# GpSimd drains behind every sixth gather, in place of a memset behind each, in a wide-and-deep recommender kernel

## The chip, the cores and the metric

The kernel runs on one core of one Trainium2 chip. The metric is the device time of one launch in microseconds (us), as the median of several runs. Times inside the kernel come from one profiled execution.

## The reference

The batch has 2048 samples. A sample has 13 dense numbers and eight categorical indices s0 to s7 into tables with 125000, 25000, 12500, 375, 375, 1000, 500 and 100 rows. Each table i has an embedding `Ei` (64 numbers a row) and a weight `wi` (one number a row). Two more weight tables, `wc0` and `wc1`, are indexed by crossed pairs of indices. Everything is float32.

```python
wide = dense @ Wd_wide
for si, wi in zip(S, w):
    wide = wide + wi[si]
wide = wide + wc0[S[3] * 375 + S[4]]
wide = wide + wc1[S[5] * 500 + S[6]]
deep_in = concatenate([dense @ Wd_deep] + [Ei[si] for Ei, si in zip(E, S)], axis=1)   # 2048 x 576
h = relu(deep_in @ W1)      # 512 wide
h = relu(h @ W2)            # 256 wide
return bias + h @ W3 + wide
```

## The kernel before, in words

The batch is cut into four blocks of 512 samples (`BLOCKS`), and each block into four tiles of 128 (`BT`), 16 tiles in all (`TILES`). Each engine has its own program, written out by hand; the engines meet only at semaphores.

**GpSimd (POOL in the profile), lines 308 to 357.** The three large tables are read by indirect DMA, here called gathers. One gather brings 128 rows, one row to a partition. For every tile there are two gathers into `x_pair` (tables 0 and 1, line 333) and one into `x_two` (table 2, line 341), so 12 for each block and 48 for the batch. After them come the gathers of single weights into `cross` (line 351): ten for the first crossed table (its first six tiles are looked up by matmul instead) and 16 for the second. That makes 74 gathers, numbered 1 to 74 in this document in the order of their issue. The first 12, those of block 0, follow one another directly. Behind each of the 61 gathers from number 13 to number 73 stands a `pause` (lines 322 to 326): it waits until the pause before it has finished, and then runs a memset of 128x320 float32 on a tile `pause_sb` that nothing reads.

**Who waits for gathers.** TensorE (PE) turns the gathered rows of block b by transposes at line 755, behind waits on `rows_gathered[b][0]` (for `x_pair`) and `rows_gathered[b][1]` (for `x_two`). VectorE (DVE) waits for all of them at lines 686 and 687, for the ten of the first crossed table at line 693, and for the 16 of the second at line 701. Line 702 then adds the last crossed weights into `result`, and SyncE stores `result` (line 305).

**The other tables.** The five small tables are looked up by matmul. DVE builds one-hot matrices in SBUF, 19 instructions of 128x512 for each block (line 517), and PE multiplies them with the tables (line 730). DVE does this for block 0 at the start, for block 1 at about 24 to 42 us, and for later blocks as their turn comes.

**The two layers.** PE multiplies in three passes (high by high, high by low, low by high: lines 786 to 788) to keep float32 accuracy. ScalarE (ACT) writes the high part of a layer's result after its relu (line 392), DVE the low part (line 542), and PE's second layer (line 819 on, called `layer2`) waits for both. At the end of the kernel ACT applies the last relu (line 401), DVE weighs it with W3 (lines 551 and 560), PE sums over the partitions (line 843, `layer3`), and DVE adds all of it up (lines 700 and 702).

Of the kernel before, what the change touches and what calls it, by code (L numbers as in the profile page):

```python
# [6 lines left out]
P = 128  # L7
# [10 lines left out]
NG, NL, NF = len(GATHERED), len(LOOKED_UP), len(FIELDS)  # L18
ROW = D + 1
CROSSES = [(3, 4), (5, 6)]  # L20
NX = len(CROSSES)
SPLIT = 3

TILES = BATCH // P
BLOCK = 512
BT = BLOCK // P
# [66 lines left out]
def program(nc, index, dense_t, big, small, small_w, wc, wc_rows, wd_rep_t, wd_wide, w1, w2, w3, bias, out):  # L93
    f32, bf16, f16, i32 = mybir.dt.float32, mybir.dt.bfloat16, mybir.dt.float16, mybir.dt.int32
# [5 lines left out]
    with ExitStack() as ctx:  # L100
        def sb(name, shape, dt):
            return ctx.enter_context(nc.sbuf_tensor(name, shape, dt))
# [4 lines left out]
        def sem(name):  # L107
            return ctx.enter_context(nc.semaphore(name))
# [63 lines left out]
        h2 = sb("h2", [P, M2, BLOCK], f32)  # L172
        wide_deep_look = [sb(f"wide_deep_look{h}", [P, BLOCK], f32) for h in range(2)]
        ones = sb("ones", [P, 1], f32)
        pause_sb = sb("pause_sb", [P, 320], f32)

        wide = sb("wide", [P, TILES], f32)
        wide_rows = sb("wide_rows", [P, TILES], f32)
# [48 lines left out]
        w2_high, w2_low = sem("w2_high"), sem("w2_low")  # L227
        rows_gathered = [[sem(f"rows_gathered{b}_{k}") for k in range(2)] for b in range(BLOCKS)]
        cross_gathered = [sem(f"cross_gathered{c}") for c in range(NX)]
        paused = sem("paused")  # L230
        onehot_ready = sem("onehot_ready")
        io_full = sem("io_full")
        io_act = sem("io_act")
# [74 lines left out]
        @block.gpsimd  # L308
        def _(pool):
            nc.gpsimd.memset(zero[:], 0.0).then_inc(zero_ready, 1)  # L310
            nc.gpsimd.iota(row_id[:], pattern=[[P, max(CHUNKS)]], base=0, channel_multiplier=1,
                           allow_small_or_imprecise_dtypes=True).then_inc(row_id_ready, 1)
            nc.gpsimd.iota(col_id[:], pattern=[[1, XPAD]], base=0, channel_multiplier=0,
                           allow_small_or_imprecise_dtypes=True).then_inc(col_id_ready, 1)
            pool.wait_ge(zero_ready, 1)
            for m in (ident16, ident):
                nc.gpsimd.affine_select(out=m[:], in_=zero[:], compare_op=ALU.not_equal, fill=1.0, base=0,
                                        pattern=[[-1, P]], channel_multiplier=1).then_inc(ident_ready, 1)
            pool.wait_ge(ident_ready, 2)
            nc.gpsimd.memset(look_w_parts[:], 0.0).then_inc(look_w_zeroed, 1)  # L320
            nc.gpsimd.memset(ones[:], 1.0).then_inc(ones_ready, 1)
            def pause(n):

                if n:
                    pool.wait_ge(paused, n)
                nc.gpsimd.memset(pause_sb[:], 0.0).then_inc(paused, 1)  # L326

            pool.wait_ge(gather_index_ready, 1)
            pauses = 0
            for b in range(BLOCKS):  # L330
                for t in range(b * BT, (b + 1) * BT):
                    for g in (0, 1):
                        nc.gpsimd.indirect_dma_start(  # L333
                            out=x_pair[:, t, g * ROW:(g + 1) * ROW], out_offset=None, in_=big[g],
                            in_offset=bass.IndirectOffsetOnAxis(ap=idx_gather[:, g, t:t + 1], axis=0),
                        ).then_inc(rows_gathered[b][0], 16)
                        if b > 0:
                            pause(pauses)
                            pauses += 1
                for t in range(b * BT, (b + 1) * BT):  # L340
                    nc.gpsimd.indirect_dma_start(  # L341
                        out=x_two[:, t, :], out_offset=None, in_=big[2],
                        in_offset=bass.IndirectOffsetOnAxis(ap=idx_gather[:, 2, t:t + 1], axis=0),
                    ).then_inc(rows_gathered[b][1], 16)
                    if b > 0:
                        pause(pauses)
                        pauses += 1
            pool.wait_ge(cross_index_ready, 1)
            for c in range(NX):
                for t in range(XTILES if c == 0 else 0, TILES):  # L350
                    nc.gpsimd.indirect_dma_start(  # L351
                        out=cross[:, c, t:t + 1], out_offset=None, in_=wc[c],
                        in_offset=bass.IndirectOffsetOnAxis(ap=idx_cross[:, c, t:t + 1], axis=0),
                    ).then_inc(cross_gathered[c], 16)
                    if (c, t) != (NX - 1, TILES - 1):
                        pause(pauses)
                        pauses += 1

        @block.scalar
        def _(act):  # L360
# [613 lines left out]
```

## Time and profile before

| what | us |
|---|---|
| three runs | 128.6, 130.53, 131.19 |
| their median | 130.53 |
| the profiled execution, its own time | 129.13 |
| its span, first to last instruction | 127.3 |
| busy in the span: PE, weight loads, POOL, DVE, ACT | 117.8, 89.2, 104.8, 80.7, 57.1 |

The span begins with the first instruction that the profile shows. All times of rows below are counted from there. The time of an execution is its span and something around it, here 1.8 us. Busy time of PE overlaps from one matmul to the next, so that the distance of their starts says more than their durations. The profile shows a gather of GpSimd for as long as GpSimd itself works at it; the transfer goes on behind it.

### The profile page before, as it was taken

The numbers are of one execution on the slowest core, as the hardware profiler recorded it, in microseconds if no ns is written. First come the engines' busy times: TensorE is split into PE (matmuls) and PEld (weight loads), VectorE is DVE, ScalarE is ACT, GpSimd is POOL, SyncE is SP. The second block draws the span as 40 slices with busy tenths as digits, with TensorE's granted clock in tenths as the row PEclk, the third lists the DMA queues.
The fourth block names the chain that finished last, engine by engine and source line by source line (L and its number), as shares of the span: only waits on it lengthen the run. The fifth ranks groups of instructions, "written<-read, shape, count | busy, mean of one in ns | idle before, by whom it ended". The sixth has DMA issues, their size and how long they took to land.

```text
span 127.3 us, 1843 instructions
## 1 busy us (share of the span) xinstructions
PE 117.8 (92%) x630; PEld 89.2 (70%) x630; DVE 80.7 (63%) x188; ACT 57.1 (45%) x100; POOL 104.8 (82%) x146
## 2 busy tenths in 40 slices
PE   6979999988999999999999999999999999999710
PEld 2443886646688885788788885787888867888710
DVE  2695996998999604975999025695995040257510
ACT  3599777456946052345462151509170432063200
POOL 6488888888899889888898888898898888888800
PEclk9999999999999999999999999999999999999965
DMA  3957766668922322223233322200000000000000
GB/s 118 344 60 248 147 178 74 133 89 323 290 21 24 26 21 21 21 19 23 21 26 20 21 20 22 21 0 0 6 0 0 0 3 0 6 0 0 0 3 0
DMA packets 6049, 7.48 MB, mean 59 GB/s; under 512 B 2755, under 2 KB 3939, under 8 KB 6040
## 3 DMA queue, kind: packets, MB, share of 16 engines
q0 software_dynamic: 2368, 1.62, 17.6%
q1 hardware_dynamic: 3240, 5.03, 12.1%
q10 hardware_dynamic: 432, 0.72, 1.6%
q8 instruction: 5, 0.08, 0.2%
q14 instruction: 4, 0.03, 0.1%
HBM read 7.17 MB, written 0.19 MB: 58 GB/s over the span
## 4 chain that ended last, share of the span: by engine, by line
POOL 79%; issue 11%; DMA 4%; POOLq 1%; DVE 1%; DVEq 0%
POOL x_pair L333 26%; POOL pause_sb L326 21%; POOL cross L351 18%; POOL x_two L341 14%; DMA idx_raw<-in_index_dram 2%; DMA cross<-in_wc_dram,idx_cross 2%; POOLq L100 1%; DVE idx_wrap L497 0%; DVE idx_sum L499 0%; DVE idx_look L502 0%; DVE result L702 0%; DVE idx_gather L502 0%; DVEq L701 0%
## 5 line engine op out<-in xcount | busy, mean ns | idle before, releaser
L517 DVE TENSOR_SCALAR onehot<-idx_bc,row_id 128x512 fp32r<-128x512 f16 x76 | 39.4, 583 | 3.7 <-PE io_ps L742 2.6
L333 POOL DMA_INDIRECT x_pair<-in_rows_dram,idx_gather x32 | 33.2, 1038 | 8.0 <-issue 6.2
L351 POOL DMA_INDIRECT cross<-in_wc_dram,idx_cross x26 | 25.4, 978 | 4.3 <-issue 4.3
L326 POOL MEMSET pause_sb<- 128x320 f32 x61 | 26.6, 437 | 0.0
L786 PE MATMUL l_ps<-xt_hi,w_hi 128*128 128x512 f32 x64 | 25.8, 404 | 0.2 <-DVE xt_lo L537 0.2
L788 PE MATMUL l_ps<-xt_hi,w_lo 128*128 128x512 f32 x64 | 25.1, 392 | 0.0
L787 PE MATMUL l_ps<-xt_lo,w_hi 128*128 128x512 f32 x64 | 25.0, 390 | 0.0
L730 PE MATMUL io_ps<-onehot,table_hl 128*128 128x512 f32 x76 | 21.0, 406 | 0.1
L375 ACT CAST xt_hi<-io_ps 64x512 fp32r<-64x512 f32 x20 | 11.6, 580 | 19.8 <-PE io_ps L730 19.6
L537 DVE TENSOR_TENSOR xt_lo<-io_ps,xt_hi 128x512 fp32r<-128x512 f32 (+1 forms) x8 | 5.5, 688 | 23.6 <-ACT xt_hi L388 23.6
L341 POOL DMA_INDIRECT x_two<-in_rows_dram,idx_gather x16 | 17.7, 1104 | 3.2 <-issue 3.2
L730 PEld LDWEIGHTS io_ps<-onehot,table_hl 128*128 128x128 f32 x76 | 14.1, 189 | 3.3 <-ACT idx_bc L363 0.3
L401 ACT ACTIVATE h<-l_ps 128x512 f32<-128x512 f32 (+1 forms) x9 | 5.0, 551 | 23.7 <-PE l_ps L788 23.7
L542 DVE SCALAR_TENSOR_TENSOR h_lo<-l_ps,h_hi 128x512 fp32r<-128x512 f32 x16 | 10.2, 683 | 6.9 <-ACT h_hi L392 6.9
L786 PEld LDWEIGHTS l_ps<-xt_hi,w_hi 128*128 128x128 f32 x64 | 12.0, 188 | 3.4 <-DVE xt_lo L537 0.6
L788 PEld LDWEIGHTS l_ps<-xt_hi,w_lo 128*128 128x128 f32 x64 | 12.0, 188 | 2.7
L787 PEld LDWEIGHTS l_ps<-xt_lo,w_hi 128*128 128x128 f32 x64 | 12.1, 188 | 2.3
L786 PE MATMUL l_ps<-h_hi,w_hi 128*128 128x512 f32 (+1 forms) x36 | 13.4, 372 | 0.1
L788 PE MATMUL l_ps<-h_hi,w_lo 128*128 128x512 f32 (+1 forms) x36 | 13.3, 370 | 0.0
L787 PE MATMUL l_ps<-h_lo,w_hi 128*128 128x512 f32 (+1 forms) x36 | 13.2, 368 | 0.0
L376 ACT CAST xt_lo<-io_ps 64x512 fp32r<-64x512 f32 x20 | 11.7, 583 | 0.5
L392 ACT ACTIVATE h_hi<-l_ps 128x512 fp32r<-128x512 f32 x16 | 9.0, 599 | 4.5 <-PE l_ps L788 3.9
(89 smaller groups left out, 132.4 us busy)
## 6 DMA issues: line engine op xcount, KB each, us to landing
idx_bc<-idx_dram SPq DMA_DIRECT2D x3, 640.0 KB, 6.2
table<-in_wc_rows_dram SPq DMA_DIRECT2D x1, 564.0 KB, 4.1
w_sb<-in_w_dram ACTq DMA_DIRECT2D x2, 256.0 KB, 4.6
x_pair<-in_rows_dram,idx_gather POOLq DMA_INDIRECT x32, 3.6
w_sb<-in_w_dram SPq DMA_DIRECT2D x2, 256.0 KB, 3.5
w_sb<-in_w_dram SPq DMA_DIRECT2D x1, 512.0 KB, 4.1
dense_stack<-dense_dram SPq DMA_DIRECT2D x3, 156.0 KB
table<-in_small_dram SPq DMA_DIRECT2D x1, 416.0 KB, 3.8
```

The source lines that it names most:

```text
L326: nc.gpsimd.memset(pause_sb[:], 0.0).then_inc(paused, 1)
L333: nc.gpsimd.indirect_dma_start(out=x_pair[:, t, g * ROW:(g + 1) * ROW], out_offset=None, in_=big[g], in_offset=bass.IndirectOffsetOnAxis(a ...
L341: nc.gpsimd.indirect_dma_start(out=x_two[:, t, :], out_offset=None, in_=big[2], in_offset=bass.IndirectOffsetOnAxis(ap=idx_gather[:, 2, t: ...
L351: nc.gpsimd.indirect_dma_start(out=cross[:, c, t:t + 1], out_offset=None, in_=wc[c], in_offset=bass.IndirectOffsetOnAxis(ap=idx_cross[:, c ...
L375: nc.scalar.copy(xt_hi[b % 2][to, g, :], bank[0:D, :]).then_inc(io_act, 1)
L376: nc.scalar.copy(xt_lo[b % 2][to, g, :], bank[D:2 * D, :]).then_inc(io_act, 1)
L517: nc.vector.tensor_scalar(onehot[:, CHUNK0[i] + c, :], idx_bc[:, b % (BLOCKS - 1), i, :], row_id[:, c:c + 1], None, ALU.is_equal).then_inc ...
L542: nc.vector.scalar_tensor_tensor(out=h1_lo[:, m, :], in0=l1_ps[m][:], scalar=0.0, in1=h1_hi[:, m, :].bitcast(f32), op0=ALU.max, op1=ALU.su ...
L730: last = nc.tensor.matmul(io_bank(use)[:], table_hl[:, c, :], onehot[:, c, :], start=c == CHUNK0[i], stop=c == CHUNK0[i] + CHUNKS[i] - 1)
L786: nc.tensor.matmul(dst, w_hi, a_hi, start=start, stop=False)
L787: nc.tensor.matmul(dst, w_hi, a_lo, start=False, stop=False)
L788: return nc.tensor.matmul(dst, w_lo, a_hi, start=False, stop=stop)
```

## The change

The tile `pause_sb` and the semaphore `paused` go, and so do the 61 memsets and the waits between them. In their place `rest` counts the gathers. Behind the gathers whose number is at least 12 (`NG * BT`, the end of block 0) and a multiple of 6, it issues one `drain` on GpSimd: behind gathers 12, 18, 24, 30, 36, 42, 48, 54, 60, 66 and 72, 11 drains in all. The gathers, their order and their semaphores stay.

```diff
-        pause_sb = sb("pause_sb", [P, 320], f32)
...
-        paused = sem("paused")
...
-            def pause(n):
-
-                if n:
-                    pool.wait_ge(paused, n)
-                nc.gpsimd.memset(pause_sb[:], 0.0).then_inc(paused, 1)
+            def rest(n):
+
+                if n >= NG * BT and n % 6 == 0:
+                    nc.gpsimd.drain()
 
             pool.wait_ge(gather_index_ready, 1)
-            pauses = 0
+            gathers = 0
             for b in range(BLOCKS):
                 for t in range(b * BT, (b + 1) * BT):
                     for g in (0, 1):
...
                         ).then_inc(rows_gathered[b][0], 16)
-                        if b > 0:
-                            pause(pauses)
-                            pauses += 1
+                        gathers += 1
+                        rest(gathers)
...
                     ).then_inc(rows_gathered[b][1], 16)
-                    if b > 0:
-                        pause(pauses)
-                        pauses += 1
+                    gathers += 1
+                    rest(gathers)
...
                     ).then_inc(cross_gathered[c], 16)
-                    if (c, t) != (NX - 1, TILES - 1):
-                        pause(pauses)
-                        pauses += 1
+                    gathers += 1
+                    rest(gathers)
```

## Rows read from the trace of the kernel before

**Rows 1.** The chain of waits that ended last: shares of the span, by line.

```profile
POOL x_pair L333 26%; POOL pause_sb L326 21%; POOL cross L351 18%; POOL x_two L341 14%; DMA idx_raw<-in_index_dram 2%; DMA cross<-in_wc_dram,idx_cross 2%; POOLq L100 1%; DVE idx_wrap L497 0%; DVE idx_sum L499 0%; DVE idx_look L502 0%; DVE result L702 0%; DVE idx_gather L502 0%; DVEq L701 0%
```

**Rows 2.** Timeline of the end: start us, us, engine, line, operation.

```profile
120.03 0.95 POOL L351 DMA_INDIRECT cross<-in_wc_dram,idx_cross  x1 [0.17 <-issue]
...
120.95 0.61 PE L843 MATMUL deep_ps<-ones,wide_deep_look 128*128 128x1 f32 x4 [0.65 <-DVE wide_deep_look L560]
121.59 0.17 DVE L700 TENSOR_TENSOR wide_deep<-wide_bias,deep_ps 128x16 f32<-128x16 f32 x1 [0.70 <-PE deep_ps L843]
122.49 0.17 DVE L702 TENSOR_TENSOR result<-wide_deep,cross 128x16 f32<-128x16 f32 x1 [0.72 <-DMA cross<-in_wc_dram,idx_cross]
```

**Rows 3.** By stretches of 10 us: length, busy of each engine, PE clock, DMA share, GB/s.

```profile
20.00:30.00 10.00, 9.46 (x75) 6.30 (x74) 8.35 (x18) 5.69 (x11) 8.43 (x12) 1.00 0.63 106
...
40.00:50.00 10.00, 10.00 (x55) 8.04 (x57) 4.93 (x10) 2.72 (x5) 8.85 (x14) 1.00 0.29 23
```

**Rows 4.** Timeline of POOL: gathers of block 0 without memsets, then with them.

```profile
4.51 1.27 POOL L333 DMA_INDIRECT x_pair<-in_rows_dram,idx_gather  x1 [1.81 <-DVE idx_gather L502]
6.09 1.17 POOL L333 DMA_INDIRECT x_pair<-in_rows_dram,idx_gather  x1 [0.30 <-issue]
...
21.61 0.94 POOL L341 DMA_INDIRECT x_two<-in_rows_dram,idx_gather  x1 [0.30 <-issue]
22.86 0.95 POOL L333 DMA_INDIRECT x_pair<-in_rows_dram,idx_gather  x1 [0.31 <-issue]
23.80 0.38 POOL L326 MEMSET pause_sb<- 128x320 f32 x1
24.35 0.95 POOL L333 DMA_INDIRECT x_pair<-in_rows_dram,idx_gather  x1 [0.16 <-issue]
25.30 0.55 POOL L326 MEMSET pause_sb<- 128x320 f32 x1
```

**Rows 5.** Timeline of DVE: one-hots in block 0, one-hots under memsets, the low part behind.

```profile
5.87 2.46 DVE L517 TENSOR_SCALAR onehot<-idx_bc,row_id 128x512 fp32r<-128x512 f16 x6 [1.05 <-ACT idx_bc L363]
...
30.70 2.54 DVE L517 TENSOR_SCALAR onehot<-idx_bc,row_id 128x512 fp32r<-128x512 f16 x5
...
33.17 2.47 DVE L542 SCALAR_TENSOR_TENSOR h_lo<-l_ps,h_hi 128x512 fp32r<-128x512 f32 x4
```

**Rows 6.** Timeline of PE: the start of layer2 of blocks 0 and 1, a turn.

```profile
33.48 0.39 PE L788 MATMUL l_ps<-xt_hi,w_lo 128*128 128x512 f32 x1
33.99 0.47 PE L786 MATMUL l_ps<-h_hi,w_hi 128*128 128x512 f32 x1
...
46.43 0.60 PE L755 MATMUL io_ps<-ident,x_pair 128*128 128x128 f32 x4
...
60.90 0.39 PE L788 MATMUL l_ps<-xt_hi,w_lo 128*128 128x512 f32 x1
61.28 0.47 PE L786 MATMUL l_ps<-h_hi,w_hi 128*128 128x512 f32 x1
```

**Rows 7.** The first operation of the kernel's own program on POOL.

```profile
0.74 0.20 POOL L310 MEMSET zero<- 128x128 f32 x1 [0.29 <-POOLq L961]
```

**Rows 8.** Issues of DMAs; the last number is the median us from issue to landing.

```profile
x_pair<-in_rows_dram,idx_gather POOLq DMA_INDIRECT x32, 3.6
...
cross<-in_wc_dram,idx_cross POOLq DMA_INDIRECT x26, 2.3
```

**Rows 9.** Timeline of PE: three-pass matmuls, the first two rows without memsets.

```profile
16.07 0.39 PE L787 MATMUL l_ps<-xt_lo,w_hi 128*128 128x512 f32 x1
...
19.02 0.39 PE L788 MATMUL l_ps<-xt_hi,w_lo 128*128 128x512 f32 x1
...
38.00 0.40 PE L786 MATMUL l_ps<-xt_hi,w_hi 128*128 128x512 f32 x1
...
40.53 0.40 PE L788 MATMUL l_ps<-xt_hi,w_lo 128*128 128x512 f32 x1
...
58.40 0.39 PE L786 MATMUL l_ps<-xt_hi,w_hi 128*128 128x512 f32 x1
```

## The prediction

> **What bounds the kernel now.** I read the chain of waits first. It puts 79% of the span on GpSimd: 26 + 18 + 14 for the three kinds of gathers and 21 for the memsets between them [rows 1]. Taken alone this says that 61 memsets cost a fifth of the time. The end of the timeline says how much of it counts. Gather 74 starts at 120.03, its data releases the last addition (L702) at 122.49. But the other chain is just as late: PE's last sums start at 120.95, and DVE adds them at 121.59 (L700) [rows 2]. So GpSimd is the last of two chains that end almost together. I then read the stretches of 10 us: PE is busy 9.46 of 10 us from 20 to 30, and 10.00 in each of the eight from 40 to 120, at a granted clock of 1.00 [rows 3]. That is the second bound. It takes no gain from GpSimd unless PE itself waited for something that the memsets delayed.
>
> **What GpSimd gains.** From gather 13 at 22.86 to gather 74 at 120.03 there are 61 steps in 97.17 us, 1.59 each [rows 2, 4]. A step is a gather of 0.95, a memset of 0.38 or 0.55, and 0.16 idle. Without a memset gathers stand 1.25 apart where DVE builds no one-hots (21.61 and 22.86, and the two steps before): 0.94 and 0.30 idle [rows 4]. Removing a memset of 0.38 therefore gives back only 0.24 where DVE is quiet. Where DVE builds one-hots, gathers of block 0 took more: 1.17 at 6.09, and the step from 4.51 to 6.09 is 1.58 [rows 4]. I price this from block 0 as a whole. Its 12 steps from 4.51 to 22.86 took 18.35 us, against 12 x 1.25 = 15.0, so 3.35 us more, in a stretch with 19 one-hots: 0.18 us for each one-hot. The other three blocks have 57, hence 10.1 us. Gather 74 would then start at 22.86 + 61 x 1.25 + 10.1 = 109.2, without the drains. The bounds are 22.86 + 76.3 = 99.1 (one-hots cost nothing) and, at block 0's own mean step of 1.53, 22.86 + 93.3 = 116.2.
>
> **What the drains cost.** The trace of before shows no drain. On POOL nothing stands behind a drain but the next gather, and behind that all later ones. Below, a drain costs nothing: GpSimd is idle 0.30 between two gathers anyway. Less than nothing is excluded, as it takes no work away. Above, it would hold the next gather until the transfers in flight have landed. That is 3.6 us after the issue of a row gather and 2.3 after one into `cross` [rows 8]; with 0.30 of idle the step becomes 3.9 or 2.6 instead of 1.25, so 2.65 or 1.35 more. I take 0.3 us, the idle time of POOL where its sequencer went from one part of the program to the next [rows 7], since all that the row shows is a sequencer that starts an empty engine again. 11 x 0.3 = 3.3, and gather 74 starts at 112.5.
>
> A drain is a different thing from a wait for data by the Trainium skill too: PSUM — Partial Sum Buffer, "Engine vs sequencer instructions", says that a drain waits for the engine to be fully idle, and Perfetto Trace Analysis, "DMA Instruction — SWDGE (GPSIMD)", that an indirect DMA is over for GpSimd when its descriptors are written, before its data has moved. By both, the low price holds and the high one does not; no run here shows it yet.
>
> **How much of this reaches the end.** Gather 74 at 112.5 lands at 114.8, before L700 at 121.59, so L702 waits for L700 alone. L700 takes 0.17, and with a few hundredths between them L702 starts at 121.81 instead of 122.49 [rows 2]: 0.68 us less. All else of the 7.5 us that GpSimd wins lies beside PE and gives nothing. GpSimd may lose 6.7 us against my figure (120.03 - 0.68 - 0.13 = 119.2, less 112.5; the 0.13 comes below) before it matters again, which is 0.6 us for each drain on top of the 0.3.
>
> **What PE gains through DVE.** The memsets slow DVE as DVE slows them. Six one-hots of block 0 took 2.46 us, 0.41 each; five under memsets took 2.54, 0.51 each [rows 5]. For 57 of them that is some 6 us of DVE. Does PE wait for it? PE is busy throughout from 40 us on [rows 3]. One place remains: layer2 of block 0 starts 0.51 behind the matmul before it (33.48 to 33.99), that of block 1 0.38 (60.90 to 61.28) [rows 6]. The low part that it needs (L542) began at 33.17, right as those five one-hots came to their end at 33.24, with no idle time of DVE before it [rows 5]: it had been queued behind them. With faster one-hots it falls to 0.38 as in the later blocks: 0.13 less. The idle PE time from 20 to 30 belongs to ACT's copies and to a DMA, which do not change. Bounds: 0 and 0.3 (to the plain distance of 0.23).
>
> The Trainium skill describes this port: SBUF — State Buffer, "SBUF: two separate sides", says that a DVE operation in a two-port mode and a GpSimd operation lock each other out for a whole instruction. The slower one-hots and the memsets of 0.55 instead of 0.38 agree. The same section says that GpSimd cannot write descriptors until such a DVE operation ends, which speaks against the change: it is the third rival below.
>
> **The sum.** 129.13 (the profiled execution) - 0.68 - 0.13 = 128.3; a step behind each chain may take some of it back, and I say 128.4. The median of the three runs is 1.4 above the profiled execution, so it matters whose spread that is. PE's chain is fixed work with no idle time. GpSimd's chain adds up 61 steps that meet DVE or do not (memsets of 0.38 or 0.55). If GpSimd is what made the runs of 130.53 and 131.19 long, PE's chain caps them all near 128.4, and the fastest run, 128.6, is such a run already. I go by that. Own range 127.8 to 129.4.
>
> **The rivals.**
> 1. The spread is not GpSimd's. Then the gain is 0.8 from 130.53: 129.7. For it: nothing in one profile shows what another run did. Against: 128.6 is so near to PE's floor.
> 2. Slower: a drain waits for landings. The place is the tail. Seven drains behind row gathers cost 2.65 and four behind `cross` 1.35: 23.9. Gather 74 then starts at 109.2 + 23.9 = 133.1, or at 123.0 if the waits swallow the cost of the one-hots. The time is 129.13 + 3.0 to 13.1, so 132 to 142, middle 137. It decides from 0.9 us a drain. PE is not starved before: gather 20, the last of block 1's `x_pair`, starts at 22.86 + 7 x 1.53 + 2 x 2.65 = 38.9, lands at 42.5, and PE turns it only at 46.43 [rows 6]. Against it: the 0.30 idle between gathers shows that GpSimd itself does not need the landing.
> 3. Slower: gathers stand still while DVE builds one-hots, now that DVE meets no memset. 57 x 0.41 = 23.4 us lost: 22.86 + 76.3 + 23.4 + 3.3 = 125.9, 5.9 late, 135.0. Against: in block 0 the gather at 6.09 ran within the burst of one-hots from 5.87 to 8.33 and took 1.17 [rows 4, 5].
> 4. Faster: the memsets write SBUF and slow PE's reads. Matmuls start 0.227 apart without memsets (13 steps from 16.07 to 19.02) and 0.230 with them (11 from 38.00 to 40.53). If that 1.3% were theirs, PE's 96 us from gather 13 to its end shrink by 1.2: 128.4 - 1.2 = 127.2. Against: they are 0.227 apart from 58.40 to 60.90 too, with memsets [rows 6, 9].
>
> **How the numbers follow.** The forecast gets 0.60, rival 1 0.17, rival 2 0.11, rival 3 0.04, rival 4 0.08. A measurement of this kernel tells about 2% from no change, so faster means below 127.9 and slower above 133.1. Faster: rival 4 and the lowest part of the forecast, 0.08 + 0.08 = 0.16. Slower: rivals 2 and 3 and a little for a drain of unforeseen price, 0.17. Within 2%: 0.67. The range goes from 127.5 to 131.0: it holds the forecast and rival 1 and leaves out most of rivals 2 to 4.
>
> **What would show it.** Right: the chain of waits of the changed kernel ends through PE, L843 and L700; gather 74 starts between 105 and 117; a gather behind a drain starts 0.3 to 0.9 behind the one before it; one-hots in later blocks take 0.48 as in block 0; L702 starts about 0.2 behind L700; layer2 of block 0 starts 0.38 behind its predecessor. Wrong: gather 74 later than 119, L702 waiting for `cross` again, steps of 3 us and more behind gathers 12, 18, 24; PE with idle time or another distance of matmuls; or a spread of runs as wide as before.

## The result, and the profile after the change

The changed kernel takes 146.81 us (median of 4 runs, 143.68 to 149.53) against 130.51 for the kernel before (median of 4 runs, 128.6 to 131.19). The ratio is 1.1134, with a 95% interval of 1.093 to 1.1338; ratios here and below leave out the executions of a kernel that took over 1.5% longer than its fastest, so this one is lower than 146.81 / 130.51. The forecast of 128.4 and its range up to 131.0 are both missed, on the side of the second rival. The profiled execution took 149.53 and is the longest of the four; sums below are made inside it.

The page of the kernel after: its span, two rows of the 40 slices, the chain of waits by engine and by line, and two groups (the columns of a group are busy us, mean ns of one, idle before).

```profile
span 147.7 us, 1793 instructions
...
PE   6799999989999999999999999999999972000000
...
POOL 5678781687187438708726852852853746737640
...
POOL 48%; issue 35%; POOLq 11%; DMA 3%; DVE 1%; DVEq 0%
POOL x_pair L330 24%; POOL cross L346 14%; POOLq L323 11%; POOL x_two L337 10%; DMA idx_raw<-in_index_dram 2%; DMA cross<-in_wc_dram,idx_cross 2%; POOLq L100 0%; DVE idx_sum L493 0%; DVE idx_wrap L491 0%; DVE idx_look L496 0%; DVE result L696 0%; DVE idx_gather L496 0%; DVEq L695 0%
...
L511 DVE TENSOR_SCALAR onehot<-idx_bc,row_id 128x512 fp32r<-128x512 f16 x76 | 31.3, 480 | 3.8 <-PE io_ps L736 2.7
...
L696 DVE TENSOR_TENSOR result<-wide_deep,cross 128x16 f32<-128x16 f32 x1 | 0.2, 174 | 21.9 <-DMA cross<-in_wc_dram,idx_cross 21.9
```

PE works without a longer pause until the 34th slice and then has nothing left, while GpSimd goes on in bursts. The memsets' 21% of [rows 1] are gone, and "issue" (time in which the engine waited for nothing that the profile shows) with 35% and POOLq (GpSimd's sequencer, here at the drains of L323) with 11% stand in their place. L696 (L702 of [rows 2]) waits 21.9 us for the gathers.

The timeline of POOL of the kernel after, around its first two drains and its ninth (columns as in [rows 2]; the bracket is the idle time before):

```profile
21.80 0.95 POOL L337 DMA_INDIRECT x_two<-in_rows_dram,idx_gather  x1 [0.30 <-issue]
27.19 2.82 POOL L330 DMA_INDIRECT x_pair<-in_rows_dram,idx_gather  x1 [4.45 <-issue]
30.32 0.95 POOL L330 DMA_INDIRECT x_pair<-in_rows_dram,idx_gather  x1 [0.30 <-issue]
...
40.93 2.77 POOL L330 DMA_INDIRECT x_pair<-in_rows_dram,idx_gather  x1 [3.32 <-issue]
...
122.67 1.08 POOL L346 DMA_INDIRECT cross<-in_wc_dram,idx_cross  x1 [2.45 <-issue]
```

Each of the eleven drains leaves a hole: 4.45, 3.32, 3.88, 3.48, 3.46, 3.64, 3.44, 3.17, 2.45, 2.42 and 2.48, together 36.2 us, where the normal idle time between gathers is 0.30 [rows 4]. The drains' own records show why. The line of the drains, cut to its first one:

```profile
L323 POOLq DRAIN  x1: 19372/19372/19372, 7.1 to 7.1; - x1
```

The sequencer of GpSimd reached it at 7.1, far ahead of the engine, and left it 19.37 later, at 26.46. That is 4.66 after the start of gather 12 (21.80), a gather into `x_two`. Its kind, in the kernel before, landed 3.5 after the issue, beside 3.6 for `x_pair` [rows 8]:

```profile
x_two<-in_rows_dram,idx_gather POOLq DMA_INDIRECT x16, 3.5
```

Gather 13 starts 0.73 after the drain's end.

The end of the kernel after:

```profile
123.68 0.17 DVE L694 TENSOR_TENSOR wide_deep<-wide_bias,deep_ps 128x16 f32<-128x16 f32 x1 [0.75 <-PE deep_ps L837]
...
143.35 0.95 POOL L346 DMA_INDIRECT cross<-in_wc_dram,idx_cross  x1 [0.30 <-issue]
145.73 0.17 DVE L696 TENSOR_TENSOR result<-wide_deep,cross 128x16 f32<-128x16 f32 x1 [21.87 <-DMA cross<-in_wc_dram,idx_cross]
```

Gather 74 starts at 143.35 instead of 120.03 [rows 2]. L694 (L700 before) is 2.1 later too, and 1.1 of that is no work of the drains: PE is already 1.6 behind at 15.40, before the first drain holds any gather back, because TensorE's granted clock is 0.63 from 8 to 10 and 0.52 from 10 to 12, where the kernel before has 1.00. The start of layer2 of block 0 is then 1.1 later than in [rows 6]. The other 1.0 falls behind PE's last three-pass matmul (120.65, before 119.67). The slices of the kernel after show the lower clock in the third:

```profile
PEclk9968999999999999999999999999999998555555
```

The last addition moved 23.2 us (from L702 to L696), the span only 20.4. So the last addition was not what ended the kernel before. The line of what closes a kernel, of the kernel before, shows what did:

```profile
L100 POOLq EVENT_SEMAPHORE  x2: 17/17/17, 127.1 to 127.2; - x2
L100 POOLq DRAIN  x1: 9140/9140/9140, 118.0 to 118.0; - x1
...
L100 SPq COMPARE_BRANCH  x1: 33/33/33, 124.1 to 124.1; - x1
```

SyncE has seen the result stored at 124.1. A drain that stands at the end of every kernel here (the closing drain) holds GpSimd until 118.0 + 9.14 = 127.1, 7.1 after gather 74 started, and everything ends at 127.3. I had read the end of the timeline only down to L702, though the chain of [rows 1] names POOLq L100.

### The profile page after: what moved, and what is told of

It is laid out like the page before. It is cut to its first block, busy times and chain, and to the rows that moved or that the text cites. A ratio compares the mean times of both kernels' runs of the same rounds, so it can differ in the third digit from the quotient of the medians.

```text
span 147.7 us, 1793 instructions
## 1 busy us (share of the span) xinstructions
PE 118.7 (80%) x630; PEld 89.5 (61%) x630; DVE 71.6 (48%) x188; ACT 56.8 (38%) x100; POOL 86.8 (59%) x85
## 4 chain that ended last, share of the span: by engine, by line
POOL 48%; issue 35%; POOLq 11%; DMA 3%; DVE 1%; DVEq 0%
POOL x_pair L330 24%; POOL cross L346 14%; POOLq L323 11%; POOL x_two L337 10%; DMA idx_raw<-in_index_dram 2%; DMA cross<-in_wc_dram,idx_cross 2%; POOLq L100 0%; DVE idx_sum L493 0%; DVE idx_wrap L491 0%; DVE idx_look L496 0%; DVE result L696 0%; DVE idx_gather L496 0%; DVEq L695 0%
## 5 line engine op out<-in xcount | busy, mean ns | idle before, releaser
L330 POOL DMA_INDIRECT x_pair<-in_rows_dram,idx_gather x32 | 42.8, 1339 | 31.6 <-issue 29.9
L511 DVE TENSOR_SCALAR onehot<-idx_bc,row_id 128x512 fp32r<-128x512 f16 x76 | 31.3, 480 | 3.8 <-PE io_ps L736 2.7
L724 PE MATMUL io_ps<-onehot,table_hl 128*128 128x512 f32 x76 | 21.8, 419 | 0.1
L337 POOL DMA_INDIRECT x_two<-in_rows_dram,idx_gather x16 | 16.7, 1041 | 4.9 <-issue 4.9
L696 DVE TENSOR_TENSOR result<-wide_deep,cross 128x16 f32<-128x16 f32 x1 | 0.2, 174 | 21.9 <-DMA cross<-in_wc_dram,idx_cross 21.9
(88 smaller groups left out, 131.0 us busy)
```

What stands on the lines that cost most here:

```text
L330: nc.gpsimd.indirect_dma_start(out=x_pair[:, t, g * ROW:(g + 1) * ROW], out_offset=None, in_=big[g], in_offset=bass.IndirectOffsetOnAxis(a ...
L337: nc.gpsimd.indirect_dma_start(out=x_two[:, t, :], out_offset=None, in_=big[2], in_offset=bass.IndirectOffsetOnAxis(ap=idx_gather[:, 2, t: ...
L511: nc.vector.tensor_scalar(onehot[:, CHUNK0[i] + c, :], idx_bc[:, b % (BLOCKS - 1), i, :], row_id[:, c:c + 1], None, ALU.is_equal).then_inc ...
L724: last = nc.tensor.matmul(io_bank(use)[:], table_hl[:, c, :], onehot[:, c, :], start=c == CHUNK0[i], stop=c == CHUNK0[i] + CHUNKS[i] - 1)
```

## The experiments

Eighteen kernels. no_rest, wait_landed, wait_then_drain, one_drain, pace_groups and drain12 are made from the kernel after, the others from the kernel before, and the diffs show the edit against that one. Each is named by its label and compared with runs of the kernel before on the same chip. one_drain, small_late_wait, memset_every2 and memset5_every6 were run once.

**no_rest: neither memsets nor drains.**

```diff
-                if n >= NG * BT and n % 6 == 0:
-                    nc.gpsimd.drain()
+                pass
```

> The changed kernel without its drains, so with neither memsets nor drains between the gathers. If the drains alone make the changed kernel slow, GpSimd ends before PE and the time is PE's floor, 128.4 us (127.8 to 129.4), a ratio of 0.98 to 1.00 to the kernel before. If gathers without memsets are themselves starved by the one-hots of DVE (rival 3), gather 74 starts after 119 us and the time is above 131 us.

Measured: 197.25 (4 runs, 181.72 to 208.59; before 130.87). Neither theory expected it: a time above 131 was to come from a late gather 74, and gather 74 is early. First the page of its profiled execution (193.85), then its stretch from 80 to 100 (columns as in [rows 3], with 20 us of length), then its longest waits (us in total, times, longest). "Remote" is what that view writes where the semaphore rose just before the wait ended, but no instruction of the core is found that raised it then.

```profile
PE   7799592747688139200008239999999999999993
...
POOL 4888777878778777777777100000000000000000
PEclk9999879555769957955555755899999999999998
DMA  5685679732233333000000000000000000000000
```

```profile
80.00:100.00 20.00, 0.00 (x0) 0.00 (x0) 0.00 (x0) 0.00 (x0) 15.12 (x17) 0.52 0.02 0
```

```profile
ACT h L394 <- remote: 48.8, 2, 41.2
...
DVE taken L594 <- remote: 33.0, 1, 33.0
PEld io_ps L748 <- issue: 24.6, 3, 23.9
```

GpSimd does what the prediction's sum said, and better: gather 74 starts at 105.31. But PE, its weight loads, DVE and ACT stand still together, for over 20 us on end at the worst, and TensorE's granted clock is 0.52 in that stretch, near its level of 1.2 GHz. I call this a stall. ACT waits 41.2 us at L394 (the relu of layer2) for a product of PE whose last matmul started at 75.74. It starts again at 112.69; GpSimd's closing drain ends at 91.3 + 21.07 = 112.4. The data itself moved: the DMA row stands at 2 to 3 tenths up to the 16th slice as in [rows 3], and no wait for a gather is among the long ones. So the memsets bought something that the profile of before cannot show: without them the *other* engines wait at semaphores whose work is done, as if the signals were held up.

**wait_landed and wait_then_drain: what a drain waits for.** At the eleven places of the drains, a wait until the data of the gathers so far has landed; the second kernel has a drain behind that wait.

```diff
                 if n >= NG * BT and n % 6 == 0:
-                    nc.gpsimd.drain()
+                    landed(n)
```

This is the edit of wait_landed; wait_then_drain keeps the drain behind `landed(n)`, a function (left out here) that waits on the semaphores of the gathers up to number n.

> Each of the 11 drains is replaced by a wait of GpSimd until all gathers issued so far have landed. Theory L (a drain waits for the landings): the idle time behind gathers 12 to 48 is like that behind the drains, 3.3 to 4.4 us, that in the crossed gathers 2.4, and the time is 142 to 148 us. Theory F (a drain has a price of its own of 2.4 to 3.5 us, whatever is in flight): the wait costs the landing alone, idle 2.6 and 1.4 us, and the time is some 8 us shorter than with drains, 135 to 139 us.

> The same waits, and behind each of them a drain, so that a drain meets a GpSimd with nothing in flight. Theory L: the drain adds less than 0.5 us in each place, the time is at most 5 us above that with waits alone. Theory F: each adds its 2.4 to 3.5 us, 26 to 38 us in all, and the time is above 160 us.

Measured: 145.07 (ratio 1.1093, 1.1055 to 1.1131) and 150.11 (1.1495, 1.1436 to 1.1555), in the main as theory L forecast. A wait for landings alone costs most of what the drains of the change cost: its eleven holes add up to 31.9 us instead of 36.2, and gather 74 starts at 135.65 instead of 143.35. But the time is not 7.7 us shorter, since the closing drain then ends 7.06 behind gather 74 instead of 2.4. POOL of wait_landed behind gather 30, its closing drain, and the drains of wait_then_drain (ns minimum, median, maximum):

```profile
61.83 1.14 POOL L345 DMA_INDIRECT x_pair<-in_rows_dram,idx_gather  x1 [2.59 <-DMA x_pair<-in_rows_dram,idx_gather]
```

```profile
L100 POOLq DRAIN  x1: 8047/8047/8047, 134.7 to 134.7; - x1
```

```profile
L339 POOLq DRAIN  x11: 527/527/1045, 28.2 to 142.8; - x11
```

With nothing in flight a drain still takes 0.527 behind six gathers and 1.045 behind the first twelve: 0.09 for each gather since the drain before. A drain thus has two parts: the landing of what is in flight, and a small price for each gather since the last drain, called its debt below. Waiting for landings does not pay the debt: the closing drain ends 7.06 or 7.07 behind gather 74 in wait_landed as in the kernel before, no_rest, small_memset, late240 and memset5_every6, whatever the distance of their gathers. PE is busy 20.00 of 20 us in each stretch of both from 40 to 120, as in the kernel after. wait_landed has two waits for "remote", of 3.1 and 2.5 us, the kernel after and wait_then_drain none.

**one_drain: how many drains the others need.**

```diff
-                if n >= NG * BT and n % 6 == 0:
+                if n == 42:
                     nc.gpsimd.drain()
```

> One drain only, behind gather 42 (at about 80 us), no memsets. By both theories GpSimd stands idle 3.3 to 3.7 us there and nowhere else over 0.3, and the time is that of the kernel without drains, since GpSimd has more than 5 us to spare. If the price of a drain comes from many drains together, the idle time is another one.

Measured: 186.46 (1 run). Two rows of its slices (4.6 us each), and its drain:

```profile
PE   7799494043000059999900390999999999999993
...
POOL 4888777778778428887777780000000000000000
```

```profile
L323 POOLq DRAIN  x1: 19407/19407/19407, 47.6 to 47.6; - x1
```

The drain ends at 67.0, 5.4 behind gather 42, and its hole is 5.16 where 3.3 to 3.7 was expected: there were 42 gathers since the start, and not six since a drain. The matmuls resume at 66.87, run for some 25 us beside new gathers, and then stop for most of the time until GpSimd is through. PE resumes 0.1 before the drain ends, so the pause in the gathers seems to free what was held, rather than the end of the drain; in no_rest some of it passed earlier too, DVE at 100.75 while gathers still went on.

**small_memset, small_late_wait, pace_groups: the rest, or how far GpSimd runs ahead?** The first keeps every wait between the memsets and makes the memset tiny. The second lets the sequencer run up to 12 memsets ahead. The third has neither memset nor drain, but waits at each group of four gathers until the group before it has landed; its semaphores by group are left out of the second diff.

```diff
-        pause_sb = sb("pause_sb", [P, 320], f32)
+        pause_sb = sb("pause_sb", [P, 8], f32)
```

```diff
+                if n < NG * TILES + NX * TILES - XTILES and n in GROUP_ENDS:
+                    k = GROUP_ENDS.index(n)
+                    if k >= 1:
+                        pool.wait_ge(landed[k - 1], 16 * GROUP_SIZE[k - 1])
```

> The kernel before with its memsets cut from 128x320 to 128x8; each still waits for the one before it. Gathers should stand about 1.25 us apart, as densely as without any rest, but GpSimd's sequencer can't run ahead. Theory R (the other engines stall because the sequencer has filled GpSimd's queue): no stall, gather 74 starts before 112 us, the time is at or below that of the kernel before, 125 to 129 us. Theory G (they stall because gathers follow one another too densely): the other engines stall as without drains, the time is over 150 us.

> The same memsets of 128x8, on 12 slots in turn, so that each waits only for the memset of 12 gathers earlier and the sequencer may run ahead until the queue is full. The spacing is that of small_memset. Theory R: the other engines stall, the time is over 150 us. Theory G: it behaves like small_memset, whichever way that goes.

> No memsets and no drains. Gathers count into a semaphore for each group of four, and GpSimd issues a group only when the group before the last has landed, at least four gathers ago. Theory R: the run-ahead stays at 8 gathers or fewer, the waits find their data landed, GpSimd ends at about 105 to 110 us, and its last drain no longer sets the end of the span: 125 to 127 us. Theory G: dense gathers stall the others, over 150 us.

Measured: 183.62 (183.12 to 184.24, ratio 1.4215), 193.06 (1 run) and 195.87 (182.59 to 199.36). In all three gathers stand 1.25 apart where DVE is quiet, and all three stall, as theory G forecast and theory R did not. Of small_memset the stretch from 60 to 80, two steps of its timeline, and its waits of POOL:

```profile
60.00:80.00 20.00, 0.00 (x0) 0.00 (x0) 0.00 (x0) 0.00 (x0) 17.03 (x32) 0.50 0.30 19
```

```profile
62.46 0.12 POOL L326 MEMSET pause_sb<- 128x8 f32 x1
62.76 0.95 POOL L333 DMA_INDIRECT x_pair<-in_rows_dram,idx_gather  x1 [0.19 <-issue]
63.71 0.12 POOL L326 MEMSET pause_sb<- 128x8 f32 x1
```

```profile
POOL pause_sb L326 <- remote: 4.2, 3, 1.6
```

Even in GpSimd's own wait of one memset for the one before it, the view shows three late releases. pace_groups keeps GpSimd's sequencer at most eight gathers ahead of the landings, and gains nothing by it. So neither the wait between memsets nor the length of the queue is what prevents the stalls. The distance of the gathers is left, and the next four kernels vary it.

**memset160, memset240, memset_every2, memset5_every6: how much rest.** The size of the memset, or the same memsets spread in another way.

```diff
-        pause_sb = sb("pause_sb", [P, 320], f32)
+        pause_sb = sb("pause_sb", [P, 240], f32)      # or 160
```

> The kernel before with memsets of 128x240 behind each gather, about 0.31 us instead of 0.38, so gathers some 1.43 us apart instead of 1.50. Theory G (a backlog grows when gathers follow faster than about one in 1.5 us): if the limit is between 1.25 and 1.43 there is no stall, GpSimd ends some 4 us earlier and its last drain with it, and the time is 2 to 4 us below that of the kernel before, 126 to 128 us. If the limit is above 1.43, the other engines stall late in the kernel and the time is above 133 us.

> Memsets of 128x160, gathers some 1.36 us apart. Limit below 1.36: no stall, GpSimd's last drain ends before the result is stored, and the time is 125 to 126 us, set by PE and the store. Limit above 1.36: stalls, above 140 us.

> Memsets of 128x320 behind every second gather only: steps of 1.25 and 1.50 in turn, 1.38 on average. If the average counts (a backlog), it behaves like memset160. If each gather needs a gap of its own, it stalls like the kernels without rests, over 170 us.

> Five memsets of 128x320 behind every sixth gather, none elsewhere: about 2.3 us in one piece, six steps in about 9.6 us, so 1.6 us on average, as dense as in the kernel before, and without a drain. If the average counts and a backlog of six gathers does no harm, there is no stall and the time is that of the kernel before, 128 to 131 us: the drains were dear only because they wait for the landing. If the landings or a drain are needed to clear the backlog, the other engines stall.

The first row is the kernel before on the chip of the four new kernels; small_memset and no_rest ran on two others, where it took 130.71 and 130.87.

| kernel | step where DVE is quiet | us | runs |
|---|---|---|---|
| before (128x320) | 1.50 | 131.03 | 130.21 to 132.98 |
| memset240 | 1.43 | 129.71 | 127.85 to 136.1, 5 runs |
| memset_every2 | 1.25 and 1.50 | 149.92 | 1 run |
| memset160 | 1.36 | 163.12 | 151.93 to 169.6 |
| small_memset | 1.25 | 183.62 | 183.12 to 184.24 |
| no_rest | 1.25 | 197.25 | 181.72 to 208.59 |

The stretch from 20 to 40 of memset240 (the run of 136.1) and of memset160:

```profile
20.00:40.00 20.00, 14.72 (x78) 9.71 (x79) 8.10 (x19) 5.45 (x10) 17.44 (x24) 0.70 0.66 143
```

```profile
20.00:40.00 20.00, 10.80 (x57) 6.31 (x57) 7.52 (x18) 4.87 (x9) 17.11 (x28) 0.83 0.70 147
```

Two waits of that execution of memset240:

```profile
DVE onehot L517 <- remote: 6.0, 1, 6.0
...
PE io_ps L755 <- DMA x_pair<-in_rows_dram,idx_gather: 2.1, 1, 2.1
```

The second of them is no stall of this kind. PE waits for gather 8, which started late (at 16.23, in the kernel before at 14.89) and was issued before any memset. Of the 5.3 us that PE is idle from 20 to 40, 1.0 are this; the stall is in the 4.3 between 28 and 40 (0.7 idle there in the kernel before). Between 1.50 and 1.36 the kernel goes from no stall over one in some executions to a loss of 32 us (163.12 against 131.03, with no single wait over 10.0). memset_every2, with 1.38 on average, lies near memset160 and far from no_rest. The ratio of memset240 is 0.9891 with an interval of 0.975 to 1.0033, which is not told from 1. memset5_every6 took 137.44 (1 run): PE kept 18.00 and 18.43 of 20 us in its first two stretches and 19.49 or more behind, so rests in lumps of five memsets seem to serve nearly as well; its loss is mostly a longer GpSimd chain, with gather 74 at 128.34 and the closing drain's end at 126.6 + 8.85 = 135.4.

**drain12: half the drains.**

```diff
-                if n >= NG * BT and n % 6 == 0:
+                if n >= NG * BT and n % 12 == 0:
                     nc.gpsimd.drain()
```

> Drains only behind gathers 12, 24, 36, 48, 60 and 72, six instead of 11. If the price of a drain is the landing plus about 0.1 us for each gather since the last one, the five drains that go give back 5 x about 2.5 us in the chain of GpSimd: some 11 to 13 us less than the changed kernel, 133 to 136 us. Theory R: a stretch of 12 gathers is at the edge of what the queue holds; if it is over it, the other engines stall in each stretch and the time is not better than with 11 drains.

Measured: 143.94 (142.84 to 145.11; ratio 1.1113, 1.0911 to 1.1315).

```profile
PE   6699949989994999269999999999699996499991
```

Gather 74 starts at 126.24, 17 us earlier than in the kernel after, but the ratio is that of the kernel after (1.1134) within its interval, where 133 to 136 us were expected. Now PE has a hole of some us in nearly every stretch of twelve close gathers, and ACT waits up to 7.7 us for "remote". Six in a row cost PE nothing that shows, twelve do.

**tail_drain, tail_drain280, tail_drain240: does the closing drain end the kernel?** Memsets up to gather 67, a drain behind 68, and nothing behind 69 to 74; the other two also have smaller memsets.

```diff
+                if n > 55:
+                    return
+                if n == 55:
+                    nc.gpsimd.drain()
+                    return
```

> Before with its memsets up to gather 67, one drain behind gather 68, and nothing behind gathers 69 to 74. Theory T (the last drain of GpSimd sets the end of before, and it takes 0.06 to 0.09 us for each gather since the drain before it, on top of the landing): gather 68 starts at 111.0 (120.03 less six steps of 1.5), gather 69 at 111.0 + 0.95 + 2.45 = 114.4, gather 74 at 120.7, the last drain ends 2.5 behind that, 123.2, instead of 127.3; the store ends at 124.7, so the span is about 125 and the time 2 us under before. Rival U (the last drain is 7.1 behind the last gather whatever went before, or something else holds the end): span 127.8, the time as before. Theory G: the last six dense gathers stall nobody, as in after.

> The same with memsets of 128x280. Steps of 1.46: gather 68 about 2 us earlier, gather 74 at 118.5. Theory G (gathers closer than about 1.43 stall the others): no stalls yet, PE ends at 121.6 as before, and its result, not GpSimd, sets the end: store done at 124, span 124.5, time 2.5 to 3 us under before. If stalls begin gradually with the distance, it is 0 to 3 us longer than that.

> The same with memsets of 128x240, which alone gave 129.7 with one run of 136. Steps of 1.43: gather 74 at 117. Theory G: now and then a stall of some us, else the span of tail_drain280, as PE sets the end of both: median 1 to 3 us under before, with a wider spread.

Measured: 132.49 (ratio 1.0157, 1.008 to 1.0235), 133.74 (1.025, 1.0159 to 1.0341) and 130.71 (1.0068, 1.0016 to 1.0119). All three were expected to be faster; each is a little slower, by less than 2% or not clear of it. POOL of tail_drain, and its closing drain:

```profile
112.80 0.95 POOL L356 DMA_INDIRECT cross<-in_wc_dram,idx_cross  x1 [0.16 <-issue]
120.11 0.95 POOL L356 DMA_INDIRECT cross<-in_wc_dram,idx_cross  x1 [6.35 <-issue]
```

```profile
L100 POOLq DRAIN  x1: 6751/6751/6751, 122.3 to 122.3; - x1
```

The closing drain did become short: it ends at 129.02, 2.66 behind gather 74 (126.36) instead of 7.1. But the new drain took the debt over. It ends at 119.38, 6.58 behind gather 68. I had priced its hole at 2.45, as behind six gathers, against my own theory, and it was 6.35 behind 68. (Gather 68 itself started 1.8 later than I had forecast.) From 6 to 68 gathers the end grows by (6.58 - 2.66) / 62 = 0.06 us for each gather. A debt can be moved, not avoided, and on the path of the gathers it costs more than behind the last one. In the profiled executions of tail_drain280 and tail_drain240 PE was busy 14.35 and 14.55 of 20 us from 20 to 40. 0.7 and 1.3 of the idle time is again the wait for gather 8; behind it DVE waits 5.0 and 4.5 for "remote". With steps of 1.46 and 1.43, stalls begin there. These two executions took 134.85 and 135.78, more than the medians, so they show that stalls occur and not how often.

**late240, early400_late240, tail_dense: is there a version faster than both?** Memsets of 128x320 (or 128x400) behind gathers 13 to 24 and 128x240 after; and the kernel before without the memsets behind gathers 68 to 73.

```diff
+                if n >= 55:
+                    return                 # tail_dense
```

> Before with memsets of 128x320 behind gathers 13 to 24 and of 128x240 from gather 25 on. Theory S (the stalls of memset240 fell between 20 and 40 us alone, while the row gathers of block 1 and the loads of the start run; later a step of 1.43 is far enough): no stall, 49 steps of 1.43 instead of 1.50, gather 74 at 116.6, the last drain ends 7.1 later at 123.7, PE's result at 121.8 and its store at 123.4; span 124 to 125, time 126 to 127 against 130.4. Rival (stalls at 1.43 come anywhere, by chance): as memset240, 128 to 136 with a wide spread. Rival V (the runs' spread is PE's and hides GpSimd's gain): within 1 us of before.

> Memsets of 128x400 behind gathers 13 to 24, 128x240 after. Theory S, and the spread of before (128.5 to 133.7) is itself small stalls between 20 and 40 us: gather 74 at 117.6, last drain ends at 124.7, span 125 to 126, time 126.5 to 128 with a narrower spread than before. If the wider rests of block 1 buy nothing: 1 us longer than late240.

> Before, without the memsets behind gathers 68 to 73. Theory T (the last drain ends the span, 7.1 behind the last gather): gather 74 at 118.6 instead of 120.03, drain ends at 125.7, time 1.4 us under before, ratio 0.989. Theory G: six close gathers could hold PE's last signals up; PE's result then comes later than 121.6, and the time is as before or above.

Measured, beside 130.16 for the kernel before: late240 129.38 (ratio 0.9931, 0.9898 to 0.9964; 126 to 127 was expected), early400_late240 129.57 (12 runs, 126.34 to 132.08), tail_dense 128.51 (128.16 to 128.89; ratio 0.9866, 0.9812 to 0.992). Stretches from 40 to 100 of late240 have PE busy throughout, so in this execution a step of 1.43 was far enough there. It wins little because gathers 25 to 74 still take 75.6 us (before 76.7): the 49 memsets add up to 18.7 instead of 21.0, one of them with 1.84, and the gathers to 48.9 instead of 47.7. early400_late240 has the widest spread of the three, against its expectation. Its profiled execution has PE busy 17.18 of 20 us from 20 to 40, but no engine waits for "remote" there: 1.55 of the 2.8 idle are the end of a wait of 2.15 for gather 8, which started at 16.70. How soon the first gathers come thus differs between executions before any rest has begun. Three of its 12 runs (126.34, 126.79, 128.08) lie below all others, and no profile shows why. tail_dense does what the closing drain's theory says, the end of its timeline and its closing drain:

```profile
119.31 1.32 POOL L353 DMA_INDIRECT cross<-in_wc_dram,idx_cross  x1 [0.30 <-issue]
...
122.95 0.17 DVE L704 TENSOR_TENSOR result<-wide_deep,cross 128x16 f32<-128x16 f32 x1
```

```profile
L100 POOLq DRAIN  x1: 16547/16547/16547, 110.2 to 110.2; - x1
```

The result is added at 122.95, and the drain ends at 126.75, 7.4 behind the last gather, in a span of 127.0. Gather 74 was forecast at 118.6. The six close gathers hold nobody up. tail_dense by 1.3% and late240 by 0.7% are faster than both kernels with an interval clear of 1 on all their runs; both gains are below the 2% that a measurement tells from no change.

## Why the prediction was wrong

**The step that failed: "I take 0.3 us" for a drain.** The bounds were right in kind. The value was taken from a row of an idle sequencer [rows 7], though the drains stand behind gathers in flight. Measured, a drain leaves (36.2 - 11 x 0.30) / 11 = 3.0 us. With gather 74 at 143.35 instead of 112.5 I was 30.8 off, and 29.6 of it are the drains (32.9 instead of 3.3). wait_landed and wait_then_drain show what the 3.0 are: mostly the landing of the gathers in flight, and a debt of 0.5 behind six gathers.

The prediction drew on the Trainium skill here: PSUM — Partial Sum Buffer, "Engine vs sequencer instructions", says that a drain waits for the engine to be fully idle. The trace agrees only if a GpSimd with gathers in flight counts as not idle: the drain ended 4.66 after the start of a gather that kept GpSimd for 0.95. The record of the gather ends before its data has moved, as the Trainium skill says in Perfetto Trace Analysis, "DMA Instruction — SWDGE (GPSIMD)"; here it is 0.95, and the landing 3.6 [rows 8]. The mistake was to join the two sentences, and to take the end of that record for idleness.

**Rival 2 had the mechanism, and was priced too low.** It said 2.65 and 1.35 a drain and 23.9 in all; measured were 3.4 (mean of the seven behind row gathers), 2.3 (the four behind `cross`) and 32.9. The landing was in it, the debt of 0.09 a gather and the 0.7 from the drain's end to the next gather were not. What stood against it, the 0.30 idle between gathers, was no evidence: gathers need no landing, drains do. With these prices rival 2 would have had gather 74 at 109.2 + 32.9 = 142.1.

**The other failure: "All else of the 7.5 us that GpSimd wins lies beside PE and gives nothing."** It prices a removed memset by its time alone. no_rest shows that drains which cost and hold back nothing would not have given 128.4 but 182 to 209: the memsets also kept the gathers apart. In the kernel after the drains do that job, six gathers at a time, and PE does not stall: it is busy 19.25 of 20 us from 20 to 40 (before 19.14) and 20.00 in each stretch to 120. The 16 us lost come from GpSimd's chain.

**"The sum" left out the closing drain.** L702 at 121.81 would have saved nothing by itself, as the kernel ended 4.6 us behind L702, with GpSimd's drain. The right path was last gather + 7.1. With gather 74 at 112.5, as I had it, that path would have been short and the store would have ended the kernel: by the 2.0 between L696 and the end of the kernel after I estimate a span of 123.7 and a time of 125.5, below my own range. So the sum was wrong in both directions, and the 128.4 was not even what its own terms give. It is also why the change lost 20.4 us of span and not 23.2: the drain behind gather 72 had paid the debt, and the store ended the kernel.

**What held.** Steps of 1.25 without memsets. One-hots: 480 ns each instead of 583, as forecast (0.48). The row of the kernel before, beside L511 above:

```profile
L517 DVE TENSOR_SCALAR onehot<-idx_bc,row_id 128x512 fp32r<-128x512 f16 x76 | 39.4, 583 | 3.7 <-PE io_ps L742 2.6
```

The cost of one-hots to gathers: from gather 12 at 21.80 to gather 74 are 62 x 1.25 + 32.9 = 110.4, and 11.2 are left for 57 one-hots, 0.20 each against my 0.18. PE's start of layer2 of block 0, of the kernel after:

```profile
34.85 0.39 PE L782 MATMUL l_ps<-xt_hi,w_lo 128*128 128x512 f32 x1
35.07 0.43 PE L780 MATMUL l_ps<-h_hi,w_hi 128*128 128x512 f32 x1
```

It starts 0.22 behind its predecessor, even better than the forecast of 0.38, the bound that I gave. Rival 4 did not happen: where matmuls stood 0.230 and 0.227 apart with memsets [rows 9], they stand 0.229 (11 steps from 39.05 to 41.57) and 0.227 apart (11 from 59.43 to 61.93) without them. Rival 3 did not in its full size: gathers were drawn out over bursts of DVE (2.82 at 27.19, 2.77 at 40.93), yet not for every one-hot, and their sum is the 11.2 above.

**What stays open.** Which resource the close gathers take from the signals of the others. Shown are that the data moves on, that waits between engines don't end though their work is done, that neither fewer gathers ahead nor a wait for the landing of the group before helps, and that distance does, or a pause behind every six, be it a drain or a wait for all landings so far. Whether it is the signals themselves that are held up is not shown. Open is also why the first twelve gathers come sooner in some executions than in others.

## What to carry to other kernels

An instruction that nothing reads may be there for its time; before it is replaced, run the kernel without it and without the replacement, because that shows what it holds back. A drain on GpSimd behind indirect DMAs cost their landing (2.3 to 3.6 us here) plus a debt of 0.04 to 0.09 us for each gather since the last drain, and every kernel here paid the last one at its end. Look past the last instruction that writes the result: what closes the kernel on each engine can be later.

## What the runs showed of the hardware that I had not expected

- Indirect DMAs of 128 rows that GpSimd issues 1.25 us apart, for some 12 or more in a row, go with waits of the other engines at semaphores of up to 41 us (no_rest); at 1.50 apart none showed, at 1.43 and 1.46 some in some executions, at 1.36 a loss of 32 us.
- A drain of GpSimd waited for its gathers to land, and with none in flight it took 0.527 us behind six and 1.045 behind twelve. A wait for their semaphores did not save that: the closing drain of wait_landed still took it all.
- The closing drain ended 7.1 us behind the last of 74 gathers, 6.6 in a drain behind 68, and 2.7 behind the last of six.
